# A one-core decoder layer: paired rotation in the first two projection panels, and several instructions placed elsewhere

## The reference, cut to what matters

```python
# 1: attention, 32 query heads, 8 key/value heads of 128
q, k, v = h @ Wq, h @ Wk, h @ Wv            # by heads
q = q * cos + rotate_half(q) * sin           # rotate_half: [-x[64:], x[:64]]
k = k * cos + rotate_half(k) * sin
attn = softmax(where(causal, q @ k.T / sqrt(128), min))
x = x + (attn @ v) @ Wo
# 2: x + fake_quant(layernorm(x)) @ fake_quant(ctx)
# 3: 64 experts of rank 8, gated by a softmax over the 16 best router scores
z = (h @ A_w.T) * gate;  x = x + (z @ B_w.T) * 2
```

## Time and profile before

| | us |
|---|---|
| median of 3 runs | 1337.99 (1337.42 to 1338.03) |
| the profiled execution | 1341.77 |
| its span | 1339.2 |
| TensorE busy | 1273.4 (95%) |
| VectorE busy | 834.3 (62%) |
| ScalarE busy | 772.0 (58%) |
| GpSimd busy | 616.7 (46%) |
| mean granted clock of TensorE | 0.988 |

### The profile page before, as it was taken

How to read it: one execution, slowest core, us unless ns; L and a number is a source line. 1 busy time by engine, 2 the same in 40 slices (tenths; PEclk the granted TensorE clock), 3 DMA queues, 4 the chain that set the end, 5 groups by cost and what they waited for, 6 DMA issues and landing times. The chain is left out here.

```text
span 1339.2 us, 19916 instructions
## 1 busy us (share of the span) xinstructions
PE 1273.4 (95%) x7016; PEld 1095.5 (82%) x7025; DVE 834.3 (62%) x1807; ACT 772.0 (58%) x1585; POOL 616.7 (46%) x454
## 2 busy tenths in 40 slices
PE   5899999999999999999999998899999999987898
PEld 4779998888888888888888877778888887676777
DVE  7787225555556655565555555446877789777763
ACT  4412237677777777777777778753333455554440
POOL 3877666678758777677775745310000000301000
PEclk9989999999999999999999999999999999998999
DMA  7033144548659568485684877788553585000001
GB/s 267 8 132 128 48 150 156 153 126 223 203 165 244 160 173 239 126 216 138 156 216 121 219 218 228 225 252 262 200 157 126 175 281 173 3 1 16 33 32 47
DMA packets 117123, 207.42 MB, mean 155 GB/s; under 512 B 10129, under 2 KB 51089, under 8 KB 113441
## 3 DMA queue, kind: packets, MB, share of 16 engines
q1 hardware_dynamic: 112992, 176.79, 40.2%
q0 software_dynamic: 4032, 29.36, 11.7%
HBM read 147.40 MB, written 88.08 MB: 176 GB/s over the span
## 5 line engine op out<-in xcount | busy, mean ns | idle before, releaser
L1229 DVE TENSOR_TENSOR pT_lo<-banks,pT_hi 128x512 fp32r<-128x512 f32 (+1 forms) x192 | 103.7, 596 | 178.7 <-ACT pT_hi L971 178.6
L1820 POOL TENSOR_TENSOR resid<-resid,colterm 128x1024 f32<-128x1024 f32 x8 | 21.4, 2677 | 281.8 <-ACT colterm L1877 181.1
L1623 PE MATMUL banks<-ob_hi,oa_hi 128*128 128x512 f32 x384 | 149.5, 389 | 1.3 <-DVE ob_lo L1266 0.9
L1623 PE MATMUL banks<-ob_lo,oa_hi 128*128 128x512 f32 x384 | 149.4, 389 | 0.0
L1623 PE MATMUL banks<-ob_hi,oa_lo 128*128 128x512 f32 x384 | 149.4, 389 | 0.0
L1581 PE MATMUL banks<-xc,nring_hi_a 128*128 128x512 f32 x448 | 140.0, 394 | 1.3 <-DVE q_made L1179 1.3
L1581 PE MATMUL banks<-xc,nring_hi_b 128*128 128x512 f32 x448 | 139.8, 393 | 0.0
L955 ACT CAST oa_hi<-oraw 128x1024 fp32r<-128x1024 f32 x48 | 50.5, 1051 | 142.6 <-PE banks L1623 138.8
L971 ACT CAST pT_hi<-banks 128x512 fp32r<-128x512 f32 (+1 forms) x192 | 86.5, 524 | 74.9 <-PE banks L1551 74.7
L1238 DVE CUSTOM_DVE_ANT_0 prob<-banks,mask 128x512 f32<-128x512 f32 (+3 forms) x256 | 109.8, 485 | 0.3 <-DVE resid L1157 0.3
L734 POOL TENSOR_TENSOR q_lo<-q_raw,q_hi 128x512 fp32r<-128x512 f32 x64 | 86.8, 1357 | 38.6 <-ACT q_hi L908 38.4
(11 more groups left out here) (245 smaller groups left out, 3489.3 us busy)
## 6 DMA issues: line engine op xcount, KB each, us to landing
q_raw<-qk_dram SPq DMA_DIRECT2D x64, 256.0 KB, 3.7
o_S<-o_st SPq DMA_DIRECT2D x64, 256.0 KB, 3.9
w<-in_L_attn_Wo SPq DMA_DIRECT2D x32, 512.0 KB, 6.7
oraw<-o_S SPq DMA_DIRECT2D x32, 512.0 KB, 3.7
nraw<-in_L_attn_Wq SPq DMA_DIRECT2D x28, 512.0 KB, 5.4
o_S<-o_S POOLq DMA_DIRECT2D x12, 1024.0 KB, 10.0
o_S<-o_N POOLq DMA_DIRECT2D x12, 1024.0 KB, 10.0
resid<-in_x SPq DMA_DIRECT2D x16, 512.0 KB, 6.1
```

The lines of the kernel that those rows point to most:

```text
L1229: nc.vector.tensor_tensor(pT[1][:, sl], turned_chunk(turned, mixed, c), as32(pT[0][:, sl]), ALU.subtract).then_inc(pT_lo, 1)
L1623: ins = nc.tensor.matmul(step_bank(m, t), oa[a][:, s % 2, k, t * P:(t + 1) * P], ob[c][:, s % 2, k, :], start=(q == 0 and k == 0 and i == ...
```

## The change

Five things are done.

1. In panels 0 and 1 the two heads of a block are no longer one tile each. The half fb = 0 of the weights takes the first 64 columns of head 0 and the last 64 of head 1, the half fb = 1 the last 64 of head 0 and the first 64 of head 1 (`turning`). So dimension d of tile 2m and the dimension that turns with it stand in one row. VectorE multiplies each tile by sin and by cos, and GpSimd subtracts and adds across the pair (`pair_sum`, placed in its queue by `PAIR_AT`). `w_high` and `w_low` of these panels are two instructions each, and a tile is stored by two transfers.
2. GpSimd's `turn_sum` for the first four waits for all of `t3`, the sums S1, S3 and S2 of panel 0 stand elsewhere in its queue, and `c00(0, 1)` stands ahead of `keep_u` on VectorE.
3. In attention `first_low` stands ahead of `k_low` and `v_low` on GpSimd, `first_high` of a unit's second step ahead of `k_high` and `v_high` on ScalarE, and `keep_first_pass` ahead of `first_weight_low` on VectorE.
4. Four accumulations that were issued in units 59, 60 and 62 and at the end of attention, and two that came after step 4 and step 16 of the output projection, are now issued after 2, 8 and 16 of its steps, two at each.
5. In the last stage `late_stats`, `late_root` and `late_scale` are done for one tile further ahead, `quantise` stands ahead of `late_scale`, `scale_tile` opens ScalarE's turn, and `turn_quantised` stands between the two halves of `expand`.

```diff
+PAIR_AT = {5: 0, 6: 1}
+PAIR_AT.update({AT[s, {"C10": "P4", "C11": "P5", "C01": "P3"}[c]] + 3: TILE_OF[s, c] // 2
+                for s, c in BLOCKS if s < TURNED and c != "C00"})
...
+    def turning(ap, fb, straight):
+        b = ap.rearrange("p (k q c) -> p k q c", k=KH, c=64)
+        return b[:, :, 2 * fb:2 * fb + 2, :] if straight else b[:, :, 1:3, :] if fb else b[:, :, 0:4:3, :]
...
+    sines = [[resid[:, t, 0:512], resid[:, t, 512:1024]] for t in (6, 2)]
...
             if s < TURNED:
-                head = (GROUPS if s else 0) + 2 * i + fb
-                sp.dma_start(qk_dram[head, j], qst[slot_of(n)]).then_inc(st[slot_of(n)], 16)
+                sp.wait_ge(pair_made, n // 2 + 1)
+                head = (GROUPS if s else 0) + 2 * i
+                for d in range(2):
+                    to = 64 * (fb if d == 0 else 1 - fb)
+                    sp.dma_start(qk_dram[head + d, j, to:to + 64], qst[slot_of(n)][64 * d:64 * d + 64, :]
+                                 ).then_inc(st[slot_of(n)], 16)
...
         def w_low(n):
             s, p = ORDER[n]
             pool.wait_ge(w_hi, n + 1)
+            if s < TURNED:
+                for fb in range(2):
+                    ins = nc.gpsimd.tensor_tensor(turning(wring[:, 1, n % 3, :], fb, True),
+                                                  turning(factor(s, p), fb, False),
+                                                  turning(as32(wring[:, 0, n % 3, :]), fb, True), ALU.subtract)
...
             if n < TPB:
-                pool.wait_ge(t3_sum, t + 1)
+                pool.wait_ge(t3_sum, TPB)
...
+        def pair_sum(m):
+            pool.wait_ge(made, 2 * m + 2)
+            x, y = qst[slot_of(2 * m)], qst[slot_of(2 * m + 1)]
+            nc.gpsimd.tensor_tensor(x, x, sines[m % 2][1], ALU.subtract)
+            nc.gpsimd.tensor_tensor(y, y, sines[m % 2][0], ALU.add).then_inc(pair_made, 1)
...
         w_low(2)
+        weight_sum(0, "S1")
         w_low(3)
-        pool.wait_ge(ln_out_v, TPB)
-        weight_sum(0, "S1")
+        for n in range(TPB):
+            turn_sum(n)
         weight_sum(0, "S3")
         weight_sum(0, "S2")
-        for n in range(2 * TPB):
+        for n in range(TPB, 2 * TPB):
             turn_sum(n)
...
             w_low(n)
+            if n in PAIR_AT:
+                pair_sum(PAIR_AT[n])
...
+            for f in steps_of(u + 1):
+                first_low(f)
             if u % 4 == 2 and half_of(u) + 1 < HALVES:
                 k_low(half_of(u) + 1)
                 v_low(half_of(u) + 1)
             for j in jobs_of(u + 2):
                 narrow_sums(j)
-            for f in steps_of(u + 1):
-                first_low(f)
-            if 2 <= u % 8 <= 4 and u >= 8:
+            if 2 <= u % 8 <= (4 if u < 56 else 2) and u >= 8:
                 accumulate_negated(u // 8 - 1, u % 8 - 2)
-            if u % 8 == 6 and u >= 32:
+            if u % 8 == 6 and 32 <= u < 56:
                 accumulate_plain(u // 8)
+        pool.wait_ge(step_done, 2)
+        accumulate_plain(GROUPS - 1)
         accumulate_negated(GROUPS - 1, 0)
-        pool.wait_ge(step_done, 4)
+        pool.wait_ge(step_done, PAIRS)
+        accumulate_negated(GROUPS - 2, 1)
         accumulate_negated(GROUPS - 1, 1)
         pool.wait_ge(step_done, 2 * PAIRS)
+        accumulate_negated(GROUPS - 2, 2)
         accumulate_negated(GROUPS - 1, 2)
...
         def rope(b, n):
-            turn = turns[n % 2]
-            if n >= 2:
-                dve.wait_ge(made, n - 1)
-            nc.vector.tensor_tensor(turn[0:64, :], b[64:128, :], sin[64:128, :], ALU.mult)
-            link(nc.vector.tensor_tensor(turn[64:128, :], b[0:64, :], sin[0:64, :], ALU.mult))
-            link(nc.vector.tensor_tensor(b, b, cos[:], ALU.mult))
-            slot_free(n)
-            nc.vector.tensor_tensor(qst[slot_of(n)], b, turn, ALU.add).then_inc(made, 1)
+            slot_free(n - n % 2)
+            slot_free(n - n % 2 + 1)
+            nc.vector.tensor_tensor(sines[n // 2 % 2][n % 2], b, sin[:], ALU.mult)
+            nc.vector.tensor_tensor(qst[slot_of(n)], b, cos[:], ALU.mult).then_inc(made, 1)
...
         for i in range(1, TT):
+            if i + 3 < TT:
+                scale_tile(i + 3)
             if i + AHEAD < TT:
                 read_product(i + AHEAD)
             high("z", i - 1)
...
-            if i + 3 < TT:
-                late_root(i + 3)
-                scale_tile(i + 3)
+            if i + 4 < TT:
+                late_root(i + 4)
...
             if i + 3 < TT:
-                late_scale(i + 3)
                 quantise(i + 3)
+            if i + 4 < TT:
+                late_scale(i + 4)
...
+            if i >= 1:
+                expand(i - 1, (0,))
             if i + 3 < TT:
                 turn_quantised(i + 3)
             if i >= 1:
-                expand(i - 1)
+                expand(i - 1, (1,))
```

More of the change, by code:

```diff
@@ L282, in attention @@
     p_done, p1_read, u_read, c11_read = sem("p_done"), sem("p1_read"), sem("u_read"), sem("c11_read")
-    made = sem("made")
+    made, pair_made = sem("made"), sem("pair_made")
     st = [sem(f"stored{n}") for n in range(4)]
@@ L344, in u_copy @@
         return resid[:, 2 + which, fb * 512:fb * 512 + 512]
-    turns = [resid[:, 6, 0:512], resid[:, 6, 512:1024]]
+    sines = [[resid[:, t, 0:512], resid[:, t, 512:1024]] for t in (6, 2)]
     qst = [resid[:, 7, 0:512], resid[:, 7, 512:1024], resid[:, 3, 0:512], resid[:, 3, 512:1024]]
@@ L353, in slot_uses @@
     def slot_uses(n):
-        return n // 4 if n < TILES - 8 else (TILES - 8) // 4 + (n - (TILES - 8)) // 2
+        return 16 * sum(2 if v < 8 * TURNED else 1 for v in range(n) if slot_of(v) == slot_of(n))
+    STORED = 16 * (2 * 2 * TURNED + (TILES - 8 - 8 * TURNED) // 4)
     def left(t, k):
@@ L466, in store @@
             i, j = int(c[1]), int(c[2])
-            sp.wait_ge(made, n + 1)
             if s < TURNED:
-                head = (GROUPS if s else 0) + 2 * i + fb
-                sp.dma_start(qk_dram[head, j], qst[slot_of(n)]).then_inc(st[slot_of(n)], 16)
+                sp.wait_ge(pair_made, n // 2 + 1)
[4 more added lines that the diff above has]
+                                 ).then_inc(st[slot_of(n)], 16)
             else:
+                sp.wait_ge(made, n + 1)
                 f0 = (s - TURNED) * 512 + i * 256
@@ L590, in _ @@
                 for n in range(4):
-                    sp.wait_ge(st[n], 16 * (TILES - 8) // 4)
+                    sp.wait_ge(st[n], STORED)
                 load_kv(0)
@@ L688, in w_low @@
             pool.wait_ge(w_hi, n + 1)
+            if s < TURNED:
[3 more added lines that the diff above has]
+                                                  turning(as32(wring[:, 0, n % 3, :]), fb, True), ALU.subtract)
+                ins.then_inc(w_lo, 1)
+                return
             nc.gpsimd.tensor_tensor(wring[:, 1, n % 3, :], factor(s, p), as32(wring[:, 0, n % 3, :]),
@@ L888, in w_high @@
                 act.wait_ge(w_sum, 4 * s + SUMS[{"P6": "S2", "P7": "S3", "P5": "S1", "P3": "S4"}[p]])
-            nc.scalar.copy(wring[:, 0, n % 3, :], factor(s, p)).then_inc(w_hi, 1)
+            if s < TURNED:
+                for fb in range(2):
+                    ins = nc.scalar.copy(turning(wring[:, 0, n % 3, :], fb, True), turning(factor(s, p), fb, False))
+                ins.then_inc(w_hi, 1)
+            else:
+                nc.scalar.copy(wring[:, 0, n % 3, :], factor(s, p)).then_inc(w_hi, 1)
         def keep_p1(s):
@@ L1058, in _ @@
                 keep_job(JOB_AT[u, 0])
+            if (u + 1, 1) in STEP_AT:
+                first_high(STEP_AT[u + 1, 1])
             if u % 4 == 2 and half_of(u) + 1 < HALVES:
@@ L1206, in read_job @@
                     for n in (2, 3):
-                        dve.wait_ge(st[n], 16 * ((TILES - 8) // 4 + 4))
+                        dve.wait_ge(st[n], STORED + 16 * 4)
                 link(nc.vector.tensor_tensor(b, b, n_p1[:], ALU.add))
@@ L1355, in _ @@
         c00(0, 0)
+        c00(0, 1)
         keep_u(0, 2, 0)
@@ L1361, in _ @@
         fill_low(27)
-        c00(0, 1)
         keep_u(0, 3, 0)
@@ L1402, in _ @@
                 if u == 1:
-                    dve.wait_ge(st[0], 16 * (TILES - 8) // 4)
-                    dve.wait_ge(st[1], 16 * (TILES - 8) // 4)
+                    dve.wait_ge(st[0], STORED)
+                    dve.wait_ge(st[1], STORED)
                 probs_low(u - 1)
@@ L1423, in _ @@
                 read_job(JOB_AT[u, 1])
+            if (u, 1) in STEP_AT and STEP_AT[u, 1] == PAIRS - 1:
+                keep_first_pass()
             if (u + 1, 0) in STEP_AT:
                 first_weight_low(STEP_AT[u + 1, 0])
-            if (u, 1) in STEP_AT and STEP_AT[u, 1] == PAIRS - 1:
-                keep_first_pass()
         probs_low(UNITS - 1)
@@ L1917, in _ @@
         copy_turned(3)
+        late_root(TPB)
         exponentials(0)
@@ L2065, in _ @@
         scale_of(2)
+        late_stats(TPB)
         gate(0)
```

(15 more changed lines are left out.)

4 lines of the change are left out of this document (1 added, 3 removed).

## The result

The changed kernel takes 1349.97 us (median of 8 runs, 1346.28 to 1351.43) against 1338.5 us for the kernel before (8 runs). The ratio is 1.007, with a 95% interval of 1.0056 to 1.0084. It is slower by 0.7%, where 0.6% faster was forecast (1329.5 us); the time lies outside the range of 1316 to 1341.

A forecast was written before the change was run, and what follows sets the result against it. TensorE, busy 95% of the span, bounds the kernel, so only its waits and slow clocks can be won. Terms +7, 0, -7.5, +1, -9 sum to -8.5 us on 1337.99: 1329.5 us, range 1316 to 1341.

The forecast's parts named there:

- Projections: Rotation in panels 0 and 1: GpSimd's queue fills with pair sums and split lows, ending the stage 7.0 us later.
- start of stage 0: New order of first weight and turn sums: (0,P6) starts within 1 us of before, counted 0 (-1 to +1.5).
- The bound of +10: Upper bound of the projections term, if each new gap brings a slow clock.
- Attention: End of attention: waits for `oa_lo` and `keep_first_pass` go, with slow clock; -7.5 us (4.1 to 8.9 less).
- the two causes named: Behind attention's 4.50 us wait: queue order, worth 1.4 us alone, and a slow `oraw` load beside an accumulation.
- As `ob_lo` is ready: In attention, the 2.66 us wait for `oa_lo` goes in full, -2.7 us, because `ob_lo` is ready.
- Output projection: Six accumulations run there instead of three; a landing going from 4.8 to 7 us costs +1 (0 to +17).
- Rival B: Accumulations crowd the output projection once an `oraw` load takes over 8.5 us: +16 instead of +1, 1344.5 us; chance 0.10.
- Last stage: Waits for `quantise` of tiles 4 to 7 go, turns of 17.8 us: -9 us (-15 to -1).
- rival C: GpSimd's addition delays VectorE in `add_product` instead of `quantise`; last stage brings -1, 1337.5 us; chance 0.12.
- Rival A: GpSimd keeps up, pair sums fit its idle time: projections bring -6.3 instead of +7, 1316 us; chance 0.13.

The follow-up runs named there:

- keep_early: The changed kernel with ScalarE's copies of the first products of panels 2 and 3 ahead of the weight casts: 1344.63 us, ratio 1.0025 to the kernel before.
- pair_later: keep_early with pair 1 summed after GpSimd's low of (0,P5) instead of ahead of it: 1341.33 us, ratio 1.0017 to the kernel before.
- only_start: The kernel before with only the new order of the first weight sums and turn sums: 1341.53 us, ratio 1.0017.
- no_pairs: The changed kernel with the rotation of panels 0 and 1 as it was before, the rest kept: 1336.86 us, ratio 0.9977 to the kernel before.
- sum_on_dve: after_fixed with the sums across a pair on VectorE instead of GpSimd: 1331.29 us, ratio 0.9932 to the kernel before.
- after_fixed: The changed kernel with keep_early, pair_later and the accumulations of S2 after output-projection steps 11 and 14: 1331.65 us, ratio 0.9938 to the kernel before.
- only_last: The kernel before with only the new order of the last stage: 1327.95 us, ratio 0.9912.
- last_att: The kernel before with the new orders in attention and the last stage, accumulations and rotation as before: 1328.3 us, ratio 0.9913.
- best_late: The kernel before with parts 3, 4 and 5, the accumulations of S2 after output-projection steps 11 and 14: 1324.51 us, ratio 0.9884.
- sum_on_dve_old: sum_on_dve with the start's old order and the copy of panel 2 back in its place: 1329.75 us, ratio 0.9916 to the kernel before.
- old_accum: The changed kernel with the accumulations issued where the kernel before issued them: 1342.44 us, ratio 1.0018 to the kernel before.
- spread: The changed kernel with the two accumulations of S2 after output-projection steps 4 and 13, not both after 8: 1346.89 us, ratio 1.0048 to the kernel before.

## Why the prediction was wrong

**Projections, +7 forecast, +15.3 measured: the step that failed.** The length of GpSimd's chain was worked out rightly: 65.0 us from pair 1 to the end of the low of (2,P6), 72.8 to 137.8, and it measured 65.0, 74.79 to 139.80. TensorE waited 2.80 us for (0,P5) where 3.2 was worked out. Two things were not. First, the chain began 2.0 us late, because the product that the second `keep_u(0,3)` reads came late, by the slow clock told below under the start of stage 0:

```profile
71.63 0.69 DVE L1178 TENSOR_TENSOR resid<-banks,raw 128x512 f32<-128x512 f32 x1 [2.03 <-PE banks L1553]
```

The earlier trace rows has that read at 69.36. Second, the prediction checked that TensorE waits for the low; it did not ask what ScalarE has queued behind a cast that waits for S2. That was `keep_p1(2)`, and it cost 5.8 us (keep_early). 7.0 + 2.0 + 5.8 is 14.8 of the 15.3 us. The bound of +10 was drawn for slow clocks after known gaps and had no room for a wait on a third engine.

By what the runs undo, the same 15.3 us divide in another way: 5.8 for the copy; 2.5 for pair 1's place (pair_later); 1 to 3 for part 2, which was counted at 0 with +1.5 as its upper end (only_start 1.1, no_pairs 3.1); what remains is 4 to 6 us, and it is put down to GpSimd's load by subtraction only. The wait of 5.2 us behind S1, S3 and S2 stands for it; with the pair sums off GpSimd (sum_on_dve against after_fixed) 1.9 us of it went, as VectorE became late in its turn.

The store that `c01(0,0)` waits for came at 103.99 (101 forecast). It was not quite harmless: `keep_u(1,2,0)` behind it let TensorE wait 0.99 us at 106.25.

**Start of stage 0, 0 forecast.** (0,P6) started at 57.06 instead of 56.37, within the forecast 1 us. `t3` fell to 2.5 us for four. But the wait of 1.98 us ahead of (0,P6), which both kernels have, was followed by a slow clock only after the change; the windows of the changed kernel show 0.58, where 56.00 to 60.00 us of before has 1.00:

```profile
57.00:61.00 4.00, 3.94 (x11) 3.12 (x12) 2.31 (x4) 0.00 (x0) 4.00 (x4) 0.58 0.01 4
```

The first 12 matmuls of (0,P6) take 4.57 us instead of 2.99, and the next ones start at 62.27 instead of 59.99, 2.3 us late. This is no chance of one execution: over the four microseconds behind that wait all nine kernels with part 2 have a clock of 0.57 to 0.69, and the five without it (before, only_last, last_att, best_late, sum_on_dve_old) have 1.00. What differs ahead of it is TensorE's wait 10 to 15 us earlier: 3.4 to 3.5 us for a turn sum near 47 us with part 2, 2.8 us near 42 us without. The forecast looked at where the stage starts and not at the clock that it starts with, and this is the 2 us by which GpSimd's chain began late.

**Attention, -7.5 forecast, -6.0 by the two traces.** Against kernels with the old attention in other executions (683.8 and 683.9) it is only -2.6. Of the two causes named, the reordering brought 1.2 us at most and the moved accumulations about 2. "As `ob_lo` is ready" did not hold: behind the earlier `oa_lo` TensorE waits for the weight low instead, 2.89 us at 824.09. The 4.50 us wait of the earlier trace rows was mostly that one execution's (only_last and only_start have the same code and not the wait), and the prediction then subtracted it from a median of which it was no part, as far as these traces tell. It had noted the 3.8 us between the profiled execution and the median, and did not ask which wait they were.

**Output projection, +1 forecast, +9.2 measured: the other step that failed.** The term of +1 rested on a piece of Wo that lands in 4.8 to 7 us; it took 11.3 us, and the two `oraw` ahead of it 10.4 and 15.0 us. Rival B had the mechanism: it named the point at which an `oraw` load takes over 8.5 us. It was given 0.10, on the ground that accumulations ran there before without a wait. But before they were issued at 890.20, 909.47 and 974.65 us, never beside the weight pieces of steps 8 to 12; the earlier trace rows had shown only 1 us of slack there. Its size (+16) was too high, since only the pair after step 8 met a stage without slack.

**Last stage, -9 forecast, -9.5 measured.** Right in its parts: two turns of 17.5 us (17.8 forecast) with TensorE never idle in them, two waits of 5.1 us in the first turn, 0.4 us of waiting for `quantise`. That three turns come so near 53.4 us is in part luck: the first of them took 18.8 us, with 0.24 us of waiting and a clock of 0.94. Of rival C a trace is there: `add_product` takes 812 ns in the mean, 750 before, 1 us in all; it cost TensorE nothing that the waits show. The prediction takes `quantise` for an example of two SBUF inputs, and it isn't one: its L1965 is a TENSOR_SCALAR with one input. That it is slow beside GpSimd is so (2.71 us; most of them take 0.69 us after the change). By only_last part 5 stands alone and brings 11 us.

**Rival A** (GpSimd keeps up) is refuted: it has no gap over 1.7 us from 74.79 to 99.68.

The sum: +15.3, -2.6, +9.2, -9.5 is +12.4 over a typical run of before; +11.5 was measured.

## What to carry to other kernels

When an engine becomes late, list not only who waits for its results but what is queued behind each of those waiters: the wait of the cast cost TensorE nothing by itself, that of the copy behind it did, and one swap was worth 5.8 us. A background transfer of 10 us may be moved only to where every load beside it has that much slack; spacing two of them helps less than choosing steps in which nothing urgent is in flight. A first stage that starts on time may still start at the slower clock, so the window behind its first wait is read too. A single long wait in a profile that lies above its median is to be checked against the median before it is counted as something to win.

## What the runs showed of the hardware

A 512 KB load with a median of 3.8 us from issue to landing took 10.4 to 15.0 us (to the cast that waited for it) beside accumulating transfers of 1 MB between DRAM buffers, which themselves took 10.3 us. Loads of x (`resid<-in_x`) were in flight too, in this kernel and in the one before; with the accumulations moved away (old_accum, best_late) the wait was gone. With two issued within 3 us of each other (917.72 and 920.17) the load took 13.5 us. VectorE's sums with both inputs in SBUF took up to 2.82 us beside GpSimd (means 1320 and 1634 ns, 690 ns alone), where its products with an input in the banks stayed at 680 to 686 ns. A gap of TensorE costs more than itself: the wait of 3.92 us for the copy was worth 5.8 us, and the stage with the one of 7.13 us is 9.2 us longer; behind both stands a stretch mostly at 1.2 GHz (0.51 and 0.54). What decides whether a gap is followed by that level stays open: the one of 3.92 us was, the one of 2.80 us was not in the changed kernel and was in spread (0.50), and the one of 1.98 us was in all nine kernels with part 2 and in none of the five others.
